# A two-layer graph network on one core: the attention mask of a pair made in four pieces, one for each block of tiles

## Chip, core and metric

The kernel runs on one core of a Trainium2 chip. The metric is the device time of one execution in microseconds (us), as the median of three runs. The profile is one more execution, taken by the hardware profiler.

## What is computed

6250 nodes with 128 features go through two graph layers over 106250 edges that are sorted by destination. The first layer is GATv2 attention, the second a gated message network:

```
h = relu(layernorm(x))
xl, xr = h @ Wl + bl, h @ Wr + br
m = leaky_relu(xl[src] + xr[dst] + edge_attr @ We, 0.2)
logits = m @ att
mx = segment_max(logits, dst)
ex = exp(logits - mx[dst])
out = segment_sum(xl[src] * ex, dst) / segment_sum(ex, dst)
...
em = relu(layer_norm(concat(x[src], x[dst]) @ msg_w + msg_b)) * edge_weight
msgs = segment_sum(em, dst) / counts
...
```

The change lies in the first layer, in the step that takes the maximum of the logits of a destination node over its own edges alone.

## The kernel before

The edges are cut into 64 chunks of 1664 (CH), each of 13 tiles of 128. A pair is one chunk with one window of 125 destination nodes (W) that its edges, sorted by destination, go to. Both layers walk the same list of pairs, 64 in this run. The 13 tiles of a pair fall into four blocks of 4, 3, 3 and 3 tiles (BLK), that is of 512, 384, 384 and 384 columns.

For every tile GpSimd (POOL) issues one indirect DMA that gathers 128 rows of the source table (gather_all, L667): 832 in each layer. They go into a ring of four pairs (xg, U = 4). POOL issues them one after the other; ahead of a block it waits until the sums of the pair four back have been taken (L662), or in the second layer until its messages have been formed.

For a pair in the attention layer, DVE first makes two things from the chunk's destination numbers (dstb, int16, 125 x 1664) and the window's node numbers (node_id, one for each partition). one_hot (L1288) writes oht, 1 in bfloat16 where an edge belongs to the node, and counts them. mask (L1296) writes nmask, 1e30 in float32 where it does not. split_rest and split_low (L1303, L1308) make parts of the window's rows for TensorE. Then the blocks run through a pipeline:

- PE forms the message of a block from oht, the window's parts and the gathered rows (gat_message: L741 three matmuls, L746 transposes that wait for the gathers).
- ACT scales it (gat_low, L982), DVE takes the maximum of both (gat_leaky, L1316), PE makes the logits (L756).
- DVE adds nmask to the logits of the block and takes the smallest over the columns in one instruction (gat_max, L1325, which reads the block's columns of nmask).
- ACT takes the exponential (L991), PE turns it (L764), ACT copies (L1000), PE adds up the sums (L774).
- For the pair two back, gat_merge (L1339 to L1345) and gat_add (L1350 to L1356) fold the results into the node's state.

Each engine's order is written out by hand in a function gat_slot, which runs over the four blocks b of pair k, some stages a few blocks behind. On DVE, slot k holds for each b: gat_leaky of block b, gat_max of the block before, and in between the preparation of pair k + 1: at b = 1 split_rest and one_hot, at b = 2 the mask, at b = 3 split_low. PE starts the messages of pair k + 1 after oht and split_low are there (L736, L737). SP loads the destination numbers of pair k + 2 into the buffer of pair k after DVE is done with the one-hot, the parts and the mask of pair k (L518 to L526). The buffers of dstb, oht and nmask are double.

The second layer has the same form (msg_slot). Its one-hot is L1291, from the same int16 numbers to bfloat16 and without the count. In place of a mask DVE makes 13 small matrices per pair, msg_prob (L1468), in runs of 7 and 6 instructions of 128 x 125.

Of the kernel before, what the change touches and what calls it, by code (L numbers as in the profile page):

```python
# [9 lines left out]
ALU = mybir.AluOpType  # L10
# [3 lines left out]
P = 128  # L14
# [20 lines left out]
BLK = [(0, 4), (4, 7), (7, 10), (10, 13)]  # L35
NB = len(BLK)
# [4 lines left out]
W = 125  # L41
NROW = N + 150
WINDOWS = -(-N // W) + 1
U = 4
# [4 lines left out]
BIG = 1e30  # L49
# [4 lines left out]
def gnn_layers(nc, a, out):  # L54
    with ExitStack() as ctx:
        def sb(name, shape, dt=F32):
            return ctx.enter_context(nc.sbuf_tensor(name, shape, dt))
# [71 lines left out]
        node_id = sb("node_id", [P, 2])  # L129
# [18 lines left out]
        def take(cols):  # L148
            lo = at[0]
            at[0] += cols  # L150
            assert at[0] <= ROOM, at[0]
            return room[:, lo:at[0]]

        xg = take(U * CH).rearrange("p (u e) -> p u e", u=U)
        dstb = take(CH).bitcast(I16).rearrange("p (u e) -> p u e", u=2)
# [5 lines left out]
        nmask = take(2 * CH).rearrange("p (u e) -> p u e", u=2)  # L161
# [180 lines left out]
        def ge(eng, s, v):  # L342
            if type(v) is not int or v > 0:
                eng.wait_ge(s, v)

        def settle(eng):
            eng.sem_inc(s_settled, 1)
# [16 lines left out]
        def turns(s, k, u, ring, n, last):  # L364

            here = (k - u) * (n // ring) + n
            return here + (last + U) * (n // ring) if s.n else here

        def nth(k, b):
            return k * NB + b  # L370

        def value(eng, ap, top):
            settle(eng)
            return nc.values_load(ap, engines=[eng.engine], min_val=0, max_val=top,
                                  skip_runtime_bounds_check_because="the list is built within these bounds")
# [11 lines left out]
        def all_pairs(eng, slot, last, tail):  # L387

            for k in range(U):
                slot(k, k, None)  # L390
            with eng.Fori(U, last, U) as k:
                for u in range(U):
                    slot(k + u, u, None)
            for u in range(U + tail):
                slot(last + u, u % U, u - U)

        def there(k, lag, end):

            if end is not None:
                return end - lag < 0  # L400
            return type(k) is not int or k - lag >= 0
# [27 lines left out]
        def _(sp):  # L429
# [42 lines left out]
            def load_rec(s, k, u):  # L472

                c = value(sp, pair_list[bass.ds(k, 1), 0:1], NCH)
                sp.dma_start(rec[:, u, :].rearrange("p (f t) -> p f t", f=3),
                             rec_rows[bass.ds(c, 1), :, :].rearrange("a f (p t) -> p (a f) t", t=T)).then_inc(s.rec[u], 16)
# [8 lines left out]
            def load_pair(n, s, k, v):  # L485
                c, b = pair_of(k)
                load_dst(s, k, v, c)
                load_window(n, s, v, b)
                return c

            def load_ew(c, v):
                sp.dma_start(oht[W:P, v, :], ew_perm[bass.ds(c, 1), :, :].rearrange("a s e -> (a s) e")).then_inc(gat.ew[v], 16)

            def state_rows(n, b):
                return state0[bass.ds(b, W), :] if n == 0 else state1[bass.ds(b, W), :]

            def width(n):
                return SW if n == 0 else D

            def feed(n, s):  # L500
                def slot(k, u, end):
                    v = u % 2
                    if there(k, 2, end):

                        b = value(sp, pair_list[bass.ds(k - 2, 1), 1:2], N)
                        if there(k, 3, end):
                            sp.wait_ge(s.kept[1 - v], turns(s, k - 3, 1 - v, 2, 16, last))
                            settle(sp)
                        sp.dma_start(st_in[0:W, v, 0:width(n)], state_rows(n, b)).then_inc(s.st[v], 16)
                    if there(k, -3, end):  # L510
                        ge(sp, s.m, nth(k - 1, NB))
                        settle(sp)
                        if n == 1:
                            ge(sp, s.pm, 2 * k)
                            settle(sp)
                        load_rec(s, k + 3, (u + 3) % U)
                    if there(k, -2, end):
                        sp.wait_ge(s.oh, k + 1)  # L518
                        settle(sp)
                        sp.wait_ge(s.split, k + 1)  # L520
                        settle(sp)
                        if n == 0:
                            sp.wait_ge(s.mask, k + 1)
                        else:
                            sp.wait_ge(s.rel, k + 1)
                        settle(sp)  # L526
                        c = load_pair(n, s, k + 2, v)
                        if n == 0:
                            sp.wait_ge(s.m, nth(k + 1, 0))
                            settle(sp)  # L530
                            load_ew(c, v)
                    if there(k, 2, end):
                        sp.wait_ge(s.state, k - 1)
                        settle(sp)
                        sp.dma_start(state_rows(n, b), st_out[0:W, v, 0:width(n)]).then_inc(s.kept[v], 16)

                all_pairs(sp, slot, last, 2)
# [562 lines left out]
        def _(dve):  # L1100
# [171 lines left out]
            def lagged(stage, k, u, b, lag, end):  # L1272
                back = -((b - lag) // NB)
                if there(k, back, end):
                    stage(k - back, (u - back) % U, (b - lag) % NB)
# [14 lines left out]
                else:  # L1290
                    dve.tensor_scalar(oht[0:W, v, :], dstb[0:W, v, :], node_id[0:W, v:v + 1], None, ALU.is_equal).then_inc(s.oh, 1)  # L1291

            def mask(k, u):
                s, v = gat, u % 2
                dve.wait_ge(s.id, k + 1)
                dve.tensor_scalar(nmask[0:W, v, :], dstb[0:W, v, :], node_id[0:W, v:v + 1], BIG, ALU.not_equal,  # L1296
                                  ALU.mult).then_inc(s.mask, 1)

            def split_rest(s, k, u):
# [5 lines left out]
            def split_low(s, k, u):  # L1305
                v = u % 2
                dve.wait_ge(s.mid, k + 1)
                dve.tensor_tensor(dws[0:W, v, 2, :], dres[0:W, :], dws[0:W, v, 1, :], ALU.subtract).then_inc(s.split, 1)  # L1308

            def gat_leaky(k, u, b):  # L1310
                s, c = gat, b % 2
                t0, t1 = BLK[b]
                cols = slice(0, (t1 - t0) * P)
                dve.wait_ge(s.low, nth(k, b) + 1)
                ge(dve, s.logit, nth(k, b) - 1)
                dve.tensor_tensor(act_m[:, c, cols], m_bank[c][:, cols], m_low[:, cols], ALU.max).then_inc(s.act, 1)  # L1316

            def gat_max(k, u, b):
                s, v = gat, u % 2
                t0, t1 = BLK[b]  # L1320
                dve.wait_ge(s.logit, nth(k, b) + 1)
                dve.wait_ge(s.mask, k + 1)
                ge(dve, s.pt, nth(k - 2, b) + 1)
                settle(dve)
                dve.tensor_tensor_reduce(neg_l[0:W, v, t0 * P:t1 * P], logit_bank[b % 2][0:W, 0:(t1 - t0) * P],  # L1325
                                         nmask[0:W, v, t0 * P:t1 * P], 1.0, BIG, ALU.add, ALU.min,
                                         nlocs[0:W, v, b:b + 1]).then_inc(s.negl, 1)
                if b == NB - 1:
                    dve.wait_ge(s.negl, nth(k, NB))
                    ge(dve, s.state, k - 3)  # L1330
                    dve.tensor_reduce(nloc[0:W, u:u + 1], nlocs[0:W, v, :], AX_X, ALU.min).then_inc(s.nloc, 1)  # L1331
# [28 lines left out]
            def gat_slot(k, u, end):  # L1360
                for b in range(NB):
                    if there(k, 0, end):
                        gat_leaky(k, u, b)
                    lagged(gat_max, k, u, b, 1, end)
                    if there(k, -1, end):
                        if b == 1:
                            split_rest(gat, k + 1, (u + 1) % U)
                            one_hot(gat, k + 1, (u + 1) % U)
                        if b == 2:
                            mask(k + 1, (u + 1) % U)  # L1370
                        if b == 3:
                            split_low(gat, k + 1, (u + 1) % U)
                    if there(k, 2, end):
                        if b == 2:
                            gat_merge(k - 2, (u - 2) % U)
                        if b == 3:
                            gat_add(k - 2, (u - 2) % U)

            split_rest(gat, 0, 0)
            one_hot(gat, 0, 0)  # L1380
            mask(0, 0)
            split_low(gat, 0, 0)
            all_pairs(dve, gat_slot, last, 2)

# [224 lines left out]
```

## Time and profile before

| | us |
|---|---|
| median of three runs | 2472.26 (2470.81 to 2472.52) |
| the profiled execution | 2471.0 |
| its span in the trace | 2469.2 |

Busy over the span: POOL 1683.3 us (68%), PE 1646.5 (67%), DVE 1522.7 (62%), PE's weight loads 1201.4 (49%), ACT 982.5 (40%). The first gather of the attention layer starts at 92.3 us, its last ends at 1166.0; those of the message layer run from 1286.0 to 2343.2. Ahead of the first lie the layer norm, the tables and the list of pairs, between them batch norm and the second tables, and behind the second the node update.

How to read it: an engine's busy time leaves out the time in which its sequencer issues and waits, so POOL with 76% busy in a layer can still be without a pause. The cost of an instruction of one engine that stands in the way of another engine's shows in the duration of the latter, not as a wait.

### The profile page before, as it was taken

The page shows a single profiled execution, that of the slowest core. Times are in us where ns is not written, and L with a number is a line of the kernel's source. Part 1 is how long each engine was busy: PE and PEld are TensorE (multiplying, and loading weights), DVE is VectorE, ACT ScalarE, POOL GpSimd, SP SyncE. Part 2 cuts the span into 40 slices and gives each one's busy share as a digit, 9 for nine tenths or more (in the row PEclk, how much of TensorE's full clock was granted, in tenths as well). Part 3 has the DMA queues.
Part 4 walks back from the last instruction along what each step waited for, and adds up shares of the span by engine and source line. Part 5 has one row for each costly group of instructions (what it writes and reads, how often), then busy time and mean ns, then how long its engine had stood idle before and what let it go on. Part 6 is the DMA issues. An engine that isn't in the chain of part 4 may idle for free.

```text
span 2469.2 us, 44266 instructions
## 1 busy us (share of the span) xinstructions
PE 1646.5 (67%) x9934; PEld 1201.4 (49%) x9934; DVE 1522.7 (62%) x4806; ACT 982.5 (40%) x3715; POOL 1683.3 (68%) x1718
## 2 busy tenths in 40 slices
PE   2387778777877777777456666666666666666650
PEld 2255555555555555555344454454454455544550
DVE  5455555555555555555647766666676666667668
ACT  3244334333434343434444444444444344434420
POOL 3377777777777777776017777777777777777732
PEclk9799889898988998999677888888788888889885
DMA  8544344444444344343244444433444444344321
GB/s 257 138 91 86 91 91 87 91 90 90 88 89 91 85 92 89 87 91 72 58 121 98 86 89 92 92 87 89 92 91 86 91 92 92 83 92 93 76 56 52
DMA packets 207823, 228.62 MB, mean 93 GB/s; under 512 B 103103, under 2 KB 153684, under 8 KB 207701
## 3 DMA queue, kind: packets, MB, share of 16 engines
q0 software_dynamic: 54784, 115.94, 24.0%
q1 hardware_dynamic: 152598, 110.34, 16.4%
q10 hardware_dynamic: 384, 1.70, 0.3%
q8 instruction: 20, 0.33, 0.1%
q14 instruction: 37, 0.30, 0.0%
HBM read 194.60 MB, written 33.24 MB: 92 GB/s over the span
## 4 chain that ended last, share of the span: by engine, by line
POOL 56%; issue 19%; PE 8%; DMA 7%; DVE 5%; SPq 1%; ACT 1%; POOLq 1%; ACTq 0%; DVEq 0%
POOL room L667 56%; DMA room<-src_table,rec 5%; PE psum L774 2%; PE psum L704 1%; PE psum L756 1%; PE psum L746 1%; DMA node_x<-in_x 1%; DVE room L1557 1%; PE psum L741 1%; DMA room<-state 1%; DVE stats L1127 1%; PE psum L835 1%; SPq L457 1%; PE psum L764 0%; ACT room L1000 0%
## 5 line engine op out<-in xcount | busy, mean ns | idle before, releaser
L667 POOL DMA_INDIRECT room<-src_table,rec x1664 | 1624.4, 976 | 684.1 <-issue 495.3
L835 PE MATMUL psum<-room,ident 128*128 128x384 f32 (+1 forms) x512 | 292.6, 659 | 377.4 <-DMA room<-src_table,rec 297.9
L1050 ACT ACTIVATE room<-psum 128x128 f32<-128x128 f32 x832 | 218.8, 274 | 585.6 <-DVE room L1478 583.2
L1316 DVE TENSOR_TENSOR room<-psum,room 128x384 f32<-128x384 f32 (+1 forms) x256 | 151.1, 590 | 455.6 <-ACT room L982 367.8
L982 ACT ACTIVATE room<-psum 128x384 f32<-128x384 f32 (+1 forms) x256 | 132.1, 516 | 560.5 <-PE psum L746 557.4
L1478 DVE TENSOR_TENSOR room<-psum,msg_g 128x384 f32<-128x384 f32 (+1 forms) x256 | 151.0, 590 | 315.0 <-PE psum L840 312.8
L746 PE MATMUL psum<-ident,room 128*128 128x128 f32 x832 | 155.4, 305 | 207.4 <-DMA room<-src_table,rec 206.9
L835 PEld LDWEIGHTS psum<-room,ident 128*128 128x128 f32 x512 | 93.1, 227 | 409.7 <-issue 384.7
L853 PE MATMUL psum<-room 128*125 128x128 f32 x1664 | 285.2, 318 | 1.5 <-ACT room L1062 1.5
L774 PE MATMUL psum<-room 128*125 128x128 f32 x1664 | 262.2, 300 | 18.9 <-ACT room L1000 6.3
L840 PEld LDWEIGHTS psum<-room 125*128 125x128 bf16 x2496 | 195.4, 112 | 140.8 <-issue 123.8
L774 PEld LDWEIGHTS psum<-room 128*125 128x125 f32 x1664 | 222.6, 204 | 56.4 <-ACT room L1000 54.5
L853 PEld LDWEIGHTS psum<-room 128*125 128x125 f32 x1664 | 248.7, 225 | 2.1 <-ACT room L1062 2.1
L1492 DVE SCALAR_TENSOR_TENSOR room<-room,rstd_e,msg_beta 128x128 f32<-128x128 f32 x832 | 243.0, 349 | 10.2
L746 PEld LDWEIGHTS psum<-ident,room 128*128 128x128 f32 x832 | 107.5, 155 | 280.5 <-DMA room<-src_table,rec 263.4
L756 PE MATMUL psum<-room,natt 128*125 128x384 f32 (+1 forms) x512 | 242.0, 557 | 1.8 <-DVE room L1316 1.8
L1468 DVE TENSOR_SCALAR room<-iota_w,rel,rec 128x125 f32<-128x125 f32 x832 | 225.2, 362 | 0.0
L840 PE MATMUL psum<-room 125*128 125x128 bf16 x2496 | 218.2, 244 | 0.0
L741 PE MATMUL psum<-room 128*128 128x384 bf16 (+1 forms) x768 | 190.5, 360 | 38.8 <-DVE room L1308 33.4
L991 ACT ACTIVATE room<-room,nloc 125x384 f32<-125x384 f32 (+1 forms) x256 | 163.8, 640 | 73.1 <-DVE nloc L1331 69.3
L1050 ACT ACTIVATION_READ_ACCUMULATOR room<-psum 128x1 f32 x832 | 168.8, 203 | 0.0
L764 PEld LDWEIGHTS psum<-ident,room 125*128 125x128 f32 x832 | 115.7, 152 | 108.0 <-issue 79.0
(179 smaller groups left out, 2122.6 us busy)
## 6 DMA issues: line engine op xcount, KB each, us to landing
room<-dst_perm SPq DMA_DIRECT2D x128, 406.2 KB
room<-src_table,rec POOLq DMA_INDIRECT x1664
room<-dst_table SPq DMA_DIRECT2D x128, 62.5 KB
src_table<-room SPq DMA_DIRECT2D x24, 224.0 KB
dst_table<-room SPq DMA_DIRECT2D x24, 224.0 KB
st_in<-state SPq DMA_DIRECT2D x64, 64.0 KB
state<-st_out SPq DMA_DIRECT2D x64, 64.0 KB
st_in<-state SPq DMA_DIRECT2D x64, 62.5 KB
```

The source lines that it names most:

```text
L667: pool.indirect_dma_start(out=xg[:, u, t * P:(t + 1) * P], out_offset=None, in_=src_table[n][:, :], in_offset=bass.IndirectOffsetOnAxis(ap ...
L741: nc.tensor.matmul(m_bank[c][:, cols], dws[:, v, p, :], oht[:, v, t0 * P:t1 * P], start=(p == 0), stop=False, skip_group_check=True)
L746: i = nc.tensor.matmul(m_bank[c][:, j * P:(j + 1) * P], xg[:, u, t * P:(t + 1) * P], ident[:, :], start=False, stop=(t == t1 - 1), is_tran ...
L756: nc.tensor.matmul(logit_bank[c][0:W, cols], natt[:, :], act_m[:, c, cols], start=True, stop=True).then_inc(s.logit, 1)
L774: i = nc.tensor.matmul(sum_bank[u % 2][0:W, 0:D], prob[:, c, t - t0, 0:W], xg[:, u, t * P:(t + 1) * P], start=(t == 0), stop=(t == T - 1), ...
L835: nc.tensor.matmul(msg_bank[b][:, cols], ident[:, :], xg[:, u, t0 * P:t1 * P], start=True, stop=False, skip_group_check=True)
L840: i = nc.tensor.matmul(msg_bank[b][:, j * P:(j + 1) * P], oht[0:W, v, t * P:(t + 1) * P], dws[0:W, v, p, :], start=False, stop=(t == t1 - ...
L853: i = nc.tensor.matmul(sum_bank[u % 2][0:W, 0:D], pm[:, u % 2, t, 0:W], zr[:, b, j * P:(j + 1) * P], start=(t == 0), stop=(t == T - 1), sk ...
L991: nc.scalar.activation(prob_wt[0:W, b % 2, 0:(t1 - t0) * P], neg_l[0:W, u % 2, t0 * P:t1 * P], ACT.Exp, bias=nloc[0:W, u:u + 1], scale=-1. ...
L1050: i = nc.scalar.activation(sq[:, j * P:(j + 1) * P], msg_bank[b][:, j * P:(j + 1) * P], ACT.Square, accum_out=var_e[:, c, j:j + 1])
L1468: i = dve.tensor_scalar(pm[:, v, t, 0:W], iota_w[:, :], rel[:, v, t:t + 1], rec[:, u, 2 * T + t:2 * T + t + 1], ALU.is_equal, ALU.mult)
L1492: i = dve.scalar_tensor_tensor(out=xz[:, c, j * P:(j + 1) * P], in0=hgs[:, c, j * P:(j + 1) * P], scalar=rstd_e[:, c, j:j + 1], in1=msg_be ...
```

## The change

mask takes a block number b and writes that block's columns alone, from the same columns of dstb. Pieces 0 and 1 (512 and 384 columns) stand at b = 2 of the slot, where the whole mask stood, pieces 2 and 3 (384 each) at b = 3, ahead of split_low. The semaphore mask now counts four for a pair. gat_max waits for its own block's piece, and SP for all four. The prologue makes the four pieces of pair 0 in a row.

```diff
--- before.py
+++ after.py
@@ -520,7 +520,7 @@
                         sp.wait_ge(s.split, k + 1)
                         settle(sp)
                         if n == 0:
-                            sp.wait_ge(s.mask, k + 1)
+                            sp.wait_ge(s.mask, nth(k + 1, 0))
                         else:
                             sp.wait_ge(s.rel, k + 1)
                         settle(sp)
@@ -1290,10 +1290,11 @@
                 else:
                     dve.tensor_scalar(oht[0:W, v, :], dstb[0:W, v, :], node_id[0:W, v:v + 1], None, ALU.is_equal).then_inc(s.oh, 1)
 
-            def mask(k, u):
+            def mask(k, u, b):
                 s, v = gat, u % 2
+                cols = slice(BLK[b][0] * P, BLK[b][1] * P)
                 dve.wait_ge(s.id, k + 1)
-                dve.tensor_scalar(nmask[0:W, v, :], dstb[0:W, v, :], node_id[0:W, v:v + 1], BIG, ALU.not_equal,
+                dve.tensor_scalar(nmask[0:W, v, cols], dstb[0:W, v, cols], node_id[0:W, v:v + 1], BIG, ALU.not_equal,
                                   ALU.mult).then_inc(s.mask, 1)
 
             def split_rest(s, k, u):
@@ -1319,7 +1320,7 @@
                 s, v = gat, u % 2
                 t0, t1 = BLK[b]
                 dve.wait_ge(s.logit, nth(k, b) + 1)
-                dve.wait_ge(s.mask, k + 1)
+                dve.wait_ge(s.mask, nth(k, b + 1))
                 ge(dve, s.pt, nth(k - 2, b) + 1)
                 settle(dve)
                 dve.tensor_tensor_reduce(neg_l[0:W, v, t0 * P:t1 * P], logit_bank[b % 2][0:W, 0:(t1 - t0) * P],
@@ -1366,8 +1367,9 @@
                         if b == 1:
                             split_rest(gat, k + 1, (u + 1) % U)
                             one_hot(gat, k + 1, (u + 1) % U)
-                        if b == 2:
-                            mask(k + 1, (u + 1) % U)
+                        if b >= 2:
+                            mask(k + 1, (u + 1) % U, 2 * b - 4)
+                            mask(k + 1, (u + 1) % U, 2 * b - 3)
                         if b == 3:
                             split_low(gat, k + 1, (u + 1) % U)
                     if there(k, 2, end):
@@ -1378,7 +1380,8 @@
 
             split_rest(gat, 0, 0)
             one_hot(gat, 0, 0)
-            mask(0, 0)
+            for b in range(NB):
+                mask(0, 0, b)
             split_low(gat, 0, 0)
             all_pairs(dve, gat_slot, last, 2)
 
```

The order of DVE at the slot's b = 2 inside the loop. Names: room is the large tile in which dstb, nmask and the like lie, st_out, st_in and shift belong to gat_merge. Before:

```order
L1325 ISA nlocs 125x1
L1296 TENSOR_SCALAR room<-room,node_id 125x1664 [waits id0]
L1339 TENSOR_TENSOR st_out<-st_in,nloc 125x1 [waits esh0,st_1,nloc0]
L1341 TENSOR_TENSOR st_out<-st_in,cloc 125x1
L1344 TENSOR_TENSOR shift<-st_out,st_in 125x1 [waits nnew0]
```

and of the change:

```order
L1326 ISA nlocs 125x1
L1297 TENSOR_SCALAR room<-room,node_id 125x512 [waits id0]
L1297 TENSOR_SCALAR room<-room,node_id 125x384 [waits id0]
L1340 TENSOR_TENSOR st_out<-st_in,nloc 125x1 [waits esh0,st_1,nloc0]
L1342 TENSOR_TENSOR st_out<-st_in,cloc 125x1
L1345 TENSOR_TENSOR shift<-st_out,st_in 125x1 [waits nnew0]
```

One instruction of 1664 columns has become two of 512 and 384, back to back, at the same place. Lines behind L1293 have moved by one.

The order of DVE at b = 3 of the same slot, where L1308 (L1309) is split_low. Before:

```order
L1316 TENSOR_TENSOR room<-psum,room 128x384 [waits logit0,low0]
L344 REGISTER_ALU [waits mask0,logit0]
L1325 ISA room,nlocs<-psum,room 125x384 [waits pt0]
L1325 ISA nlocs 125x1
L1308 TENSOR_TENSOR room<-room 125x128 [waits mid0]
L1350 TENSOR_REDUCE den<-dens 125x1 [waits sum0]
```

and of the change:

```order
L1317 TENSOR_TENSOR room<-psum,room 128x384 [waits logit0,low0]
L344 REGISTER_ALU [waits mask0,logit0]
L1326 ISA room,nlocs<-psum,room 125x384 [waits pt0]
L1326 ISA nlocs 125x1
L1297 TENSOR_SCALAR room<-room,node_id 125x384 [waits id0] x2
L1309 TENSOR_TENSOR room<-room 125x128 [waits mid0]
L1351 TENSOR_REDUCE den<-dens 125x1 [waits sum0]
```

Two instructions of 384 columns now stand ahead of split_low. The orders of the other engines are the same in both.

## Rows read from the trace of the kernel before

**Rows 1.** Busy time of POOL's gathers by layer (windows of line L667): count in brackets

```profile
core 0: us, POOL busy (x), PEclk, DMA share, GB/s
92.20:1166.10 1073.90, 820.46 (x832) 0.91 0.41 89
1285.90:2343.30 1057.40, 803.96 (x832) 0.83 0.41 90
```

**Rows 2.** Line L667 in the attention layer: duration ns min/median/max; idle time before by cause

```profile
L667 POOL DMA_INDIRECT room<-src_table,rec x832: 940/944/1782, 92.3 to 1165.1; - x167
...
  issue: 245.3, 805
...
  PE psum L774: 7.9, 26
```

**Rows 3.** Line L667 in the message layer, same columns

```profile
L667 POOL DMA_INDIRECT room<-src_table,rec x832: 940/944/1350, 1286.0 to 2342.3; - x167
...
  issue: 249.9, 820
```

**Rows 4.** Groups of DVE by form: busy us, mean ns | idle before

```profile
L1468 DVE TENSOR_SCALAR room<-iota_w,rel,rec 128x125 f32<-128x125 f32 x832 | 225.2, 362 | 0.0
L1288 DVE TENSOR_SCALAR_CACHE_REDUCE room<-room,node_id 125x1664 bf16<-125x1664 int16 x64 | 124.6, 1946 | 2.3
...
L1291 DVE TENSOR_SCALAR room<-room,node_id 125x1664 bf16<-125x1664 int16 x64 | 42.4, 662 | 2.3
```

**Rows 5.** Lines of DVE, each by itself: duration ns min/median/max, first and last start

```profile
L1296 DVE TENSOR_SCALAR room<-room,node_id x64: 1078/1083/1298, 110.6 to 1149.8; 125x1664 f32<-125x1664 int16 x64
...
L1291 DVE TENSOR_SCALAR room<-room,node_id x64: 652/654/719, 1301.2 to 2325.4; 125x1664 bf16<-125x1664 int16 x64
...
L1468 DVE TENSOR_SCALAR room<-iota_w,rel,rec x832: 327/341/545, 1301.9 to 2333.3; 128x125 f32<-128x125 f32 x167
```

**Rows 6.** Timeline (start us, us, engine line): a gather that starts inside a mask

```profile
527.72 1.08 DVE L1296 TENSOR_SCALAR room<-room,node_id 125x1664 f32<-125x1664 int16 x1
...
527.97 1.65 POOL L667 DMA_INDIRECT room<-src_table,rec  x1 [0.30 <-issue]
...
528.71 0.15 DVE L1339 TENSOR_TENSOR st_out<-st_in,nloc 125x1 f32<-125x1 f32 x1
```

**Rows 7.** Timeline: a gather that was under way when the mask started

```profile
512.29 1.62 POOL L667 DMA_INDIRECT room<-src_table,rec  x1 [0.30 <-issue]
...
512.71 1.08 DVE L1296 TENSOR_SCALAR room<-room,node_id 125x1664 f32<-125x1664 int16 x1
```

**Rows 8.** Timeline: a gather half done when the mask starts, and the next

```profile
159.42 0.94 POOL L667 DMA_INDIRECT room<-src_table,rec  x1 [0.30 <-issue]
...
159.91 1.30 DVE L1296 TENSOR_SCALAR room<-room,node_id 125x1664 f32<-125x1664 int16 x1
...
160.66 1.36 POOL L667 DMA_INDIRECT room<-src_table,rec  x1 [0.30 <-PE psum L774]
```

**Rows 9.** Timeline, message layer: a gather that starts inside L1291

```profile
1309.54 0.65 DVE L1291 TENSOR_SCALAR room<-room,node_id 125x1664 bf16<-125x1664 int16 x1
1309.83 1.18 POOL L667 DMA_INDIRECT room<-src_table,rec  x1 [0.30 <-issue]
```

**Rows 10.** Timeline, message layer: a gather inside a run of seven L1468

```profile
1650.21 1.86 DVE L1468 TENSOR_SCALAR room<-iota_w,rel,rec 128x125 f32<-128x125 f32 x7
...
1650.95 0.95 POOL L667 DMA_INDIRECT room<-src_table,rec  x1 [0.30 <-issue]
```

**Rows 11.** Timeline: end of a slot, from gat_max to the next pair's first matmuls

```profile
619.12 0.92 PE L774 MATMUL psum<-room 128*125 128x128 f32 x6
...
619.58 0.29 DVE L1308 TENSOR_TENSOR room<-room 125x128 bf16<-125x128 f32 x1
...
620.06 0.82 PE L741 MATMUL psum<-room 128*128 128x512 bf16 x3
```

**Rows 12.** Waits of the attention layer (108 to 1160 us): us in total, times, longest

```profile
PE psum L746 <- DMA room<-src_table,rec: 205.7, 111, 5.3
```

## Prediction

> **What bounds the kernel now.** I first read the gathers by layer [rows 1]. POOL issues 832 in each; busy time is 820.5 us in the attention layer, 986 ns each, and 804.0 in the message layer, 966 each. Beside that stand the pauses [rows 2]: 0.30 us ahead of each gather (245.3/805), all of them the sequencer's own; the 26 put down to PE are as short (7.9/26). 832 x 0.305 is 253.8, and 820.5 + 253.8 = 1074.3, which is the layer's whole stretch of 1073.9. So POOL issues without one pause from 92.3 to 1166.1 us, everything else in the layer follows it, and a nanosecond off a gather there is a nanosecond off the kernel. What follows starts when the layer is done, so it moves along.
>
> The gathers should all be alike: least 940, median 944 ns, yet the longest takes 1782 [rows 2]. 832 x 0.944 is 785.4, so 35.1 us are excess. The message layer has 18.6 of it and a longest of 1350 [rows 3].
>
> The timeline says where the excess is. At 527.97 a gather starts 0.25 us into a mask and takes 1.65 us [rows 6]. One that was 0.42 us old when the mask began takes 1.62 [rows 7]. One that was 0.49 old takes 0.94, but there the mask takes 1.30 in place of 1.08, and the next gather, 0.75 us into the mask, takes 1.36 [rows 8]. So the mask and the gathers exclude each other for a time. I went through all 64 masks, from 110.6 to 1149.8 us, this way: 90 gathers overlap one, with 33.7 us above 943 ns between them, 0.53 per mask. The other 742 have 2.2 us in all. Nearly all of the layer's excess comes from this one instruction.
>
> **What an instruction costs the gathers.** The rows give rules, with D an instruction's duration. A gather that starts over 0.1 us after it ends at its end + 0.82: 528.80 + 0.82 = 529.62 in [rows 6], 161.21 + 0.82 = 162.03 in [rows 8], and for L1291 1310.19 + 0.82 = 1311.01 in [rows 9]. Its loss is D - y - 0.12, y being how late it starts. A gather that is x old at that time, x under 0.45, ends at the instruction's end + 0.12 (513.79 + 0.12 = 513.91 in [rows 7]); its loss is x + D - 0.82. A gather older than that loses nothing. The worst loss is about D - 0.22, and below a D of 0.37 the second kind vanishes. With the gathers' period of 1.25 us and phases spread evenly, the mean for D = 1.08 comes to 0.51 us; 0.53 was found. The cost grows nearly with the square of D.
>
> How long will a piece be? The fp32 mask of 1664 columns takes 1.083, L1291 with bfloat16 output 0.654 and the counting L1288 1.946 [rows 4, 5]. These fit 0.225 + 0.858, 0.225 + 0.429 and 0.225 + 1.716: a fixed part, and columns at 1, 2 and 1/2 of the mask's rate. A piece of 512 then takes 0.225 + 0.264 = 0.489, one of 384 0.225 + 0.198 = 0.423. The next instruction starts 0.09 before the end (528.71 against 528.80 in [rows 6]).
>
> To price a piece I use what three lines cost the gathers, by the column part h: L1296, h = 0.858, 0.53 us each; L1291, h = 0.429, 9.4 us over 64, 0.147 each; L1468, h near 0.065, 6.05 us over 832, 0.0073 each. A curve a h + b h^2 through the first two has a = 0.07, b = 0.63 and gives 0.0072 for the third, which it wasn't fitted to. So 384 columns cost 0.039, 512 cost 0.063.
>
> L1468 also answers the question whether pieces back to back act as one long hold. It comes in runs of 7 that last 1.86 us, and a gather in the middle of one takes 0.95 [rows 10]; its durations reach 545 ns against 341 [rows 5], so it does exclude gathers but lets them in between two instructions.
>
> The Trainium skill, SBUF — State Buffer, "SBUF: two separate sides", has a rule for this: GpSimd and a VectorE instruction in a 2-port mode share a port pair that whoever starts first keeps for its whole instruction, and the other waits. The trace agrees on the exclusion. It doesn't agree on "whole": a gather past its middle isn't stopped [rows 8]. What the page's rule would give is the second rival.
>
> **The sum.** *Removed:* 64 masks at 0.527 = 33.7 us of POOL's path. *Added:* per pair 0.063 + 3 x 0.039 = 0.18, times 64 = 11.5 us. The bounds are 0 (every piece falls where it harms nothing) and 18.9 (each two pieces as one hold: h = 0.462 and 0.396 by the curve, 0.168 + 0.128 = 0.296 per pair). I take 11.5, since [rows 10] are the nearest to pieces in a run. Net -22.2 us.
>
> *DVE:* start to start the mask took 0.99; the pieces take 0.40 + 3 x 0.33 = 1.39, so 0.40 x 64 = 26 us more. DVE is busy 587 of the layer's 1074 us and waits for what the gathers bring; its cover is that. *Moved:* 0.67 us of mask now stand ahead of split_low, on which PE's next pair hangs. In [rows 11] split_low ends at 619.87 and PE starts the pair at 620.06, having been busy until 620.04; now it would start near 620.7. That is 0.67 x 64 = 43 us of PE, covered by the 205.7 us in which PE waits for gathers [rows 12], 3.2 per pair, and by the ring, which lets POOL run on some ten blocks ahead of the sums. If that cover were gone, the 43 us would be on the path. *SP:* it waits for the last piece in place of the mask, but it already waited for split_low of the same pair, which stands behind both; its loads start 0.67 us later, a slot (16 us) ahead of their use. Nothing. *Waits:* gat_max waits for its own piece, made most of a slot earlier. Nothing. *Prologue:* 0.4 us of DVE once, while POOL gathers. Nothing.
>
> The profiled execution took 2471.0 (its span 2469.2): 2471.0 - 22.2 = 2448.8. The median of the runs is 1.3 above it: **2450 us**. Bounds alone: 33.7 - 18.9 and 33.7 - 0 give 2457.5 and 2438.6.
>
> **Rivals.** *Two pieces hold as one.* For: they follow each other on DVE with nothing in between. Against: [rows 10]. 2457.5. Chance 0.11.
>
> *Each piece stops gathers for its whole length.* Then a gather that starts in a piece waits until its end, and the loss is D^2/2 over the period: (0.489^2 + 3 x 0.423^2)/2.5 = 0.31 per pair, 19.9 us, against 1.083^2/2.5 = 0.47, 30.0 us, for the mask: 10.1 us less, 2462. (This is the rule of the Trainium skill's page named above.) Against: it gives 30.0 where the trace has 33.7, and [rows 8]. Chance 0.08.
>
> *The pieces don't run as the mask did.* A piece of 384 at half the mask's rate, that of L1288, would take 0.62 and exclude nothing, as L1288 does (its gathers are among the 742): 2439. Against: the pieces have even counts and the same types as the mask. Chance 0.03.
>
> *The pieces keep step with the gathers: slower.* DVE's work in a block starts when the block's last gather has landed, so the phase needn't be spread evenly. If each of the four pieces starts just before a gather does, each costs D - 0.22: 0.27 + 3 x 0.20 = 0.87 per pair, 56 us against 33.7, so +22 us, 2494. It turns slower above 0.13 us per piece, three times my mean. Against: in the masks of [rows 6 to 8] the phases differ (0.25 after, 0.42 and 0.49 before), and four pieces at two places can't all be unlucky for long. Chance 0.06.
>
> *PE becomes the bound*: the 43 us don't vanish in its waits, because these are uneven (up to 5.3 us at a time). POOL would then show pauses, and the gain would be eaten: about 2472, or a little more. Against: the ring's depth. Chance 0.05.
>
> **How the numbers follow.** Forecast 0.67. Faster by over 0.2% (4.9 us, about what a measurement of this kernel can tell from no change) are the forecast and the first three rivals: 0.67 + 0.11 + 0.08 + 0.03 = 0.89. The last rival gives 0.04 to the same and 0.01 to slower, with the one before it 0.07. The range goes from the bound at 2439 to the second rival at 2462, and leaves out some 0.12.
>
> **What to look for.** Gathers of the attention layer: busy 798 us in place of 820.5, mean 960 ns; the longest, 1782, gone, and nothing above 1.3. POOL's stretch 1052 us, its pauses still 0.30. Pieces of about 0.42 and 0.49 us, some stretched by gathers. PE's wait for gathers lower by some 40 to 65 us. The message layer unchanged at 804. Wrong would be: gathers of 1.5 us around two pieces (held as one), pauses on POOL above 0.31 (PE's), or a stage 1074 us long in spite of shorter gathers.

## Result and profile after

| | before | after |
|---|---|---|
| median of four runs, us | 2471.53 | 2443.57 (2442.83 to 2448.17) |
| span of the profiled execution | 2469.2 | 2441.0 |

The ratio is 0.9892, with a 95% interval of 0.9875 to 0.9909: the kernel is 1.1% faster. 2450 was predicted, 2439 to 2462 the range. Among the experiments below, one of the six executions of mask_on_act took 2470.9 us at a mean granted TensorE clock of 0.63; the other five had 0.85 and took 2438.0 to 2442.2, and the one widens that kernel's interval.

The windows of POOL's gathers, each layer from its first to its last, answer to [rows 1]:

```profile
core 0: us, POOL busy (x), PEclk, DMA share, GB/s
91.30:1138.80 1047.50, 794.03 (x832) 0.92 0.42 91
1257.90:2313.60 1055.70, 802.20 (x832) 0.82 0.41 90
```

The attention layer's 832 gathers take 794.0 us in place of 820.5, and the layer is as much shorter: 1047.5 against 1073.9. The message layer, in which nothing was edited, differs by 1.8 us. These two are the 28.2 us of the span.

Line L667 in the attention layer, with its idle time by cause, against [rows 2]:

```profile
L667 POOL DMA_INDIRECT room<-src_table,rec x832: 940/944/1191, 91.4 to 1137.7; - x167
...
  issue: 246.2, 808
...
  PE psum L774: 7.0, 23
```

The median gather is the same, 944 ns; the longest fell from 1782 to 1191. The pauses are still 0.30 us each, so POOL still sets the pace. The excess (busy time above that of as many undisturbed gathers) over 832 x 0.944 = 785.4 fell from 35.1 to 8.6 us.

The pieces, as a line of DVE (duration ns min/median/max):

```profile
L1297 DVE TENSOR_SCALAR room<-room,node_id x256: 399/416/652, 110.6 to 1126.2; 125x512 f32<-125x512 int16 x64, 125x384 f32<-125x384 int16 x64
```

And the timeline with a gather inside the first of two pieces, DVE's row and POOL's:

```profile
893.24 0.81 DVE L1297 TENSOR_SCALAR room<-room,node_id 125x512 f32<-125x512 int16 x2
...
893.42 1.11 POOL L667 DMA_INDIRECT room<-src_table,rec  x1 [0.30 <-issue]
```

The first piece alone takes 0.48 us, from 893.24 to 893.72, and 893.72 + 0.82 = 894.54 against the gather's end at 894.53. It is the rule of [rows 6], with the end of the first piece: the second doesn't count. Inside a whole mask a gather that started 0.25 us late took 1.65.

What PE waited for, gathers and then split_low (L1309), against [rows 11, 12] (us in total, times, longest):

```profile
PE psum L746 <- DMA room<-src_table,rec: 157.3, 98, 5.6
...
PE psum L741 <- DVE room L1309: 54.8, 26, 34.3
```

And the wait for split_low in the kernel before:

```profile
PE psum L741 <- DVE room L1308: 33.4, 1, 33.4
```

PE's waits for gathers shrank by 48 us. The long wait for split_low is the one at the layer's start, 33.4 us before and 34.3 now. The other 25 waits, 20.5 us in all, are new. So the late split_low is real, and POOL's unchanged pauses show that it is covered.

### The profile page after: what moved, and what is told of

Its sections match the earlier page's. It is cut to its first block, busy times and chain, and to the rows that moved or that the text cites. A ratio compares the mean times of both kernels' runs of the same rounds, so it can differ in the third digit from the quotient of the medians.

```text
span 2441.0 us, 44458 instructions
## 1 busy us (share of the span) xinstructions
PE 1632.4 (67%) x9934; PEld 1191.2 (49%) x9934; DVE 1554.4 (64%) x4998; ACT 979.6 (40%) x3715; POOL 1655.1 (68%) x1718
## 4 chain that ended last, share of the span: by engine, by line
POOL 55%; issue 19%; PE 9%; DMA 8%; DVE 5%; ACT 1%; SPq 1%; POOLq 1%; ACTq 0%; DVEq 0%
POOL room L667 55%; DMA room<-src_table,rec 5%; PE psum L704 2%; PE psum L774 2%; PE psum L835 1%; PE psum L746 1%; DMA node_x<-in_x 1%; DVE room L1560 1%; PE psum L756 1%; DVE stats L1127 1%; PE psum L840 1%; DMA room<-state 1%; PE psum L741 1%; PE psum L853 0%; ACT room L1000 0%
## 5 line engine op out<-in xcount | busy, mean ns | idle before, releaser
L667 POOL DMA_INDIRECT room<-src_table,rec x1664 | 1596.2, 959 | 683.1 <-issue 496.2
L853 PEld LDWEIGHTS psum<-room 128*125 128x125 f32 x1664 | 249.9, 226 | 1.5 <-ACT room L1062 1.5
L774 PEld LDWEIGHTS psum<-room 128*125 128x125 f32 x1664 | 216.4, 199 | 56.5 <-ACT room L1000 52.6
L741 PE MATMUL psum<-room 128*128 128x384 bf16 (+1 forms) x768 | 185.2, 352 | 79.6 <-DVE room L1309 54.8
```

The lines of the kernel that those rows point to most:

```text
L667: pool.indirect_dma_start(out=xg[:, u, t * P:(t + 1) * P], out_offset=None, in_=src_table[n][:, :], in_offset=bass.IndirectOffsetOnAxis(ap ...
L741: nc.tensor.matmul(m_bank[c][:, cols], dws[:, v, p, :], oht[:, v, t0 * P:t1 * P], start=(p == 0), stop=False, skip_group_check=True)
L774: i = nc.tensor.matmul(sum_bank[u % 2][0:W, 0:D], prob[:, c, t - t0, 0:W], xg[:, u, t * P:(t + 1) * P], start=(t == 0), stop=(t == T - 1), ...
L853: i = nc.tensor.matmul(sum_bank[u % 2][0:W, 0:D], pm[:, u % 2, t, 0:W], zr[:, b, j * P:(j + 1) * P], start=(t == 0), stop=(t == T - 1), sk ...
```

## Experiments

All kernels below share one edit outside the loops: the two counts that are loaded at the start are checked against their bounds.

```diff
-            turns_left = nc.values_load(counts[0:1, 0:1], engines=[eng.engine], min_val=NCH - 3 * U, max_val=NCH * WINDOWS,
-                                        skip_runtime_bounds_check_because="each chunk has 1 to WINDOWS pairs")
+            turns_left = nc.values_load(counts[0:1, 0:1], engines=[eng.engine], min_val=NCH - 3 * U, max_val=NCH * WINDOWS)
```

and likewise for the count of blocks. With it the line numbers move by one or two. The kernels were run in three groups on three chips, those of the first two groups once each, and chips differ: the kernel before took 2471.2 us beside whole_bounded to thirteen_pieces, 2467.6 beside four_at_2 to message_counted, and 2474.1 beside the last three. So the comparisons go by the traces of the two layers first, and by the total second.

One more difference has to be known when busy times are compared. In most traces the median gather takes 944 ns. In before_split_low_late, message_counted, mask_on_act and mask_on_act_message_counted it takes 947, in both layers, for no reason that the edits give. This is mask_on_act's line in the attention layer:

```profile
L666 POOL DMA_INDIRECT room<-src_table,rec x832: 941/947/1073, 92.9 to 1133.9; - x167
```

Over 832 gathers these 3 ns are 2.5 us of busy time that belong to no DVE instruction.

### whole_bounded: the base

> The kernel before, with the two loaded counts (pairs, blocks) checked against their bounds once per engine ahead of the loops; every further kernel has this too, so this is their base. Every theory: no difference. Gathers of the attention layer busy 820 us (818 to 823), of the message layer 804, time within 3 us of the kernel before.

2470.1 us, beside 2471.2 for the kernel before on the same chip. Gathers busy 819.8 and 802.4 us. The check costs nothing that can be seen.

### counted_mask: a whole mask in the counting form

```diff
-                dve.tensor_scalar(nmask[0:W, v, :], dstb[0:W, v, :], node_id[0:W, v:v + 1], BIG, ALU.not_equal,
-                                  ALU.mult).then_inc(s.mask, 1)
+                dve.tensor_scalar(nmask[0:W, v, :], dstb[0:W, v, :], node_id[0:W, v:v + 1], None, ALU.not_equal, ALU.add,
+                                  accum_out=mcount[0:W, :]).then_inc(s.mask, 1)
```

> The whole mask in one instruction at its old place, but in the form of L1288 (compare and count): it writes 0 and 1 in place of 0 and 1e30, so the output isn't the reference's. It takes DVE 1.95 us in place of 1.08. Theory (an instruction at double rate shuts the gathers out while it runs, one in the counting form doesn't): the excess falls from 35 to about 2 us, gathers of the attention layer busy 788 us, time about 2437, below even the four pieces, although DVE works longer than in either. Rival (what counts is how long DVE is busy, or how long one of its instructions is, whatever its form): excess above 35 us, about 60, busy about 845, time 2495.

2437.4 us. The windows of its gathers in both layers, its line L666, and the timeline of one mask with two gathers:

```profile
92.70:1132.10 1039.40, 786.07 (x832) 0.93 0.43 92
1253.10:2308.10 1055.00, 801.66 (x832) 0.84 0.41 90
```

```profile
L666 POOL DMA_INDIRECT room<-src_table,rec x832: 940/944/1062, 92.7 to 1131.1; - x167
```

```profile
122.80 1.94 DVE L1295 TENSOR_SCALAR_CACHE_REDUCE room<-room,node_id 125x1664 f32<-125x1664 int16 x1
...
122.83 0.94 POOL L666 DMA_INDIRECT room<-src_table,rec  x1 [0.30 <-issue]
124.07 0.94 POOL L666 DMA_INDIRECT room<-src_table,rec  x1 [0.30 <-issue]
```

An instruction with the same input and the same shape and type of output, nearly twice as long, and two gathers pass through it at 0.94 us each. Excess 0.7 us. Length alone doesn't stop the gathers; it counts only in a form that does. That settles where the 35 us came from; the layer's floor is 786.

### two_pieces

```diff
-            def mask(k, u, b):
+            def mask(k, u, h):
                 s, v = gat, u % 2
-                cols = slice(BLK[b][0] * P, BLK[b][1] * P)
+                cols = slice(0, 896) if h == 0 else slice(896, CH)
...
                         if b >= 2:
-                            mask(k + 1, (u + 1) % U, 2 * b - 4)
-                            mask(k + 1, (u + 1) % U, 2 * b - 3)
+                            mask(k + 1, (u + 1) % U, b - 2)
```

(The waits of gat_max and SP and the prologue count two pieces in place of four.)

> Two pieces of 896 and 768 columns, the first at b = 2, the second at b = 3. Theory (cost by the length of one hold, by the curve of the prediction): 0.168 + 0.128 us per pair, 19 us in all, busy about 805 us, time about 2455. If two pieces back to back held as one, this would be the same as the four pieces measured (busy 794). If the gain came from taking DVE work out of b = 2 and not from short holds, busy also about 794.

2448.7 us, its gathers and its pieces:

```profile
93.50:1145.70 1052.20, 798.73 (x832) 0.92 0.42 91
```

```profile
L1295 DVE TENSOR_SCALAR room<-room,node_id x128: 610/681/851, 111.6 to 1132.8; 125x896 f32<-125x896 int16 x64, 125x768 f32<-125x768 int16 x64
```

Between one piece and four, as the theory has it: 798.7 us of gathers, 4.7 above the four. But the excess is 13.3 us where the curve gave 19, and the time is 6 us below the expected 2455: the curve is too high in its middle.

### thirteen_pieces

```diff
-                dve.tensor_scalar(nmask[0:W, v, cols], dstb[0:W, v, cols], node_id[0:W, v:v + 1], BIG, ALU.not_equal,
-                                  ALU.mult).then_inc(s.mask, 1)
+                for t in range(*BLK[b]):
+                    i = dve.tensor_scalar(nmask[0:W, v, t * P:(t + 1) * P], dstb[0:W, v, t * P:(t + 1) * P], node_id[0:W, v:v + 1], BIG,
+                                          ALU.not_equal, ALU.mult)
+                i.then_inc(s.mask, 1)
```

(The line that sets cols goes too.)

> Thirteen pieces of 128 columns, 7 at b = 2 and 6 at b = 3. Theory: the column part of one is 0.066 us, like L1468's, at 0.0075 us each 0.1 per pair, 6 us in all; busy 788 to 792. DVE's mask costs 13 x 0.21 = 2.7 us per pair in place of 1.4, of which 1.3 ahead of split_low, in place of 0.67; if PE's waits cover it, time 2438 to 2442. Rival (more instructions, more meetings with a gather, each at a fixed price): 13/4 of the excess of the four pieces, 28 us, busy 813, time 2463. Rival (PE becomes the bound by the late split_low): pauses above 0.31 us on POOL, time above 2450 with busy at 790.

2440.9 us:

```profile
92.80:1136.20 1043.40, 790.06 (x832) 0.89 0.43 92
```

```profile
L1295 DVE TENSOR_SCALAR room<-room,node_id x832: 266/281/505, 110.6 to 1124.8; 125x128 f32<-125x128 int16 x167
```

Three times as many instructions as the change, and the excess is 4.7 us in place of 8.6. A fixed price per meeting is out: it would have been 28.

### four_at_2: do pieces back to back hold as one?

```diff
-                        if b >= 2:
-                            mask(k + 1, (u + 1) % U, 2 * b - 4)
-                            mask(k + 1, (u + 1) % U, 2 * b - 3)
+                        if b == 2:
+                            for c in range(NB):
+                                mask(k + 1, (u + 1) % U, c)
```

> The change with all four pieces in one run at b = 2, none ahead of split_low. Theory (each piece is a hold by itself, gathers get in between, also within a run of four): by the rules of the prediction 0.16 us per pair, against 0.15 for the change's two runs of two; busy of the attention layer's gathers 793 to 797, time within 3 us of the change. Rival (back to back they shut the gathers out as one): their hold would be as long as that of the whole mask, busy about 825 to 840, time about 2475 to 2490. If the lateness of split_low had cost the change anything, this one would be faster than it with the same busy time.

2440.1 us. Its two layers:

```profile
92.60:1139.00 1046.40, 793.06 (x832) 0.91 0.42 91
1258.60:2310.60 1052.00, 798.56 (x832) 0.84 0.42 90
```

Four in a run are no worse than two and two: 793.1 against 794.0. So gathers do get in between two pieces; what shortens the hold is the cut, not the distance. The total is 3.5 us below the change's median, 0.5 more than expected, but the message layer, which has no edit, is 3.7 us shorter (1052.0 against 1055.7). Over the runs without an edit there its gathers' busy time varies from 798.6 to 804.0 us. The attention layers are alike (1046.4 and 1047.5), so where split_low stands cost the change nothing that can be seen.

### before_split_low_late and change_split_low_3us: the cover on PE

```diff
                         if b == 3:
+                            for _ in range(1):
+                                dve.tensor_reduce(idle[0:PP, :], node_x[:, 0:4, :].rearrange("p t f -> p (t f)"), AX_X, ALU.max)
                             split_low(gat, k + 1, (u + 1) % U)
```

(0:21 in place of 0:4 for the second, on top of the change.)

> The kernel before (whole mask) with one more DVE instruction ahead of split_low in each slot, a maximum over 512 columns of node_x that nothing uses, about 0.7 us: it puts split_low off as the change does and does nothing else. Theory (PE's waits for gathers cover it): POOL's pauses stay at 0.30, time within 2 us of the kernel before. Rival (the late split_low costs part of the change's gain): up to 0.7 x 64 = 43 us slower, POOL pauses above 0.31.

2474.6 us, where the kernel before took 2467.6 beside it and whole_bounded 2470.1 on another chip: outside the 2 us that were expected. But the trace has its attention layer as it was:

```profile
94.00:1167.70 1073.70, 820.25 (x832) 0.91 0.41 89
1287.90:2345.10 1057.20, 803.68 (x832) 0.83 0.42 90
```

1073.7 and 1057.2 us, against 1073.9 and 1057.4 in [rows 1]. The span, 2472.8, is 3.6 us longer than that of the kernel before: 1.8 of them lie ahead of the first gather and 1.8 behind the last, where the edit doesn't reach. The run of 2467.6 has no trace, so where the rest of the 7 us lies isn't known. The extra instruction took 0.68 us. So a split_low that much later costs nothing in the layer, though the time alone doesn't show it.

> The change with such an instruction over 2688 columns, about 3.0 us, ahead of split_low: the point from which that wait decides. PE waits 157 us for gathers in the changed kernel, 2.5 us per pair, of which the mean is used up by 3.0. Theory (cover by PE's waits plus the ring of four pairs): the overshoot of some 0.5 us per pair costs at most 32 us, and the ring takes some of it up: 2446 to 2476, with pauses on POOL for the first time. Rival (there is much more cover than PE's waits show): within 2 us of the change, no pauses. Rival (little cover): 3.0 x 64 = 190 us, 2630.

2477.0 us. The extra instruction takes 2.94 us. Its windows, its gathers' causes, and the wait between the layers:

```profile
91.60:1146.20 1054.60, 792.91 (x832) 0.87 0.42 90
1295.90:2349.30 1053.40, 800.07 (x832) 0.83 0.41 90
```

```profile
POOL room L666 <- PE psum L773: 16.9, 38, 1.8
...
PE psum L740 <- DVE room L1308: 139.5, 30, 32.9
```

```profile
POOL room L666 <- DMA rec<-rec_rows: 149.8, 1, 149.8
```

The gathers themselves are as short as the change's (792.9), yet the run is 33.5 us slower than the change, and 37 slower than four_at_2 on the same chip. POOL now pauses for PE's sums, up to 1.8 us, and the layer grows by 7 us. The greater part is not there: between the layers POOL waits 149.8 us, where the change has 119.4. PE's last sums (L773) end 42 us after the last gather, where in the change they end 14 us after it: PE has fallen 28 us further behind. It waits for no gather any more. With 2.9 us more the cover is gone; with the change's 0.7 it is not. The time is 1 us above the expected range, which had counted on POOL's pauses to show the loss.

### message_counted

```diff
-                if s is gat:
-                    dve.tensor_scalar(oht[0:W, v, :], dstb[0:W, v, :], node_id[0:W, v:v + 1], None, ALU.is_equal, ALU.add,
-                                      accum_out=cloc[0:W, u:u + 1]).then_inc(s.oh, 1)
-                else:
-                    dve.tensor_scalar(oht[0:W, v, :], dstb[0:W, v, :], node_id[0:W, v:v + 1], None, ALU.is_equal).then_inc(s.oh, 1)
+                dve.tensor_scalar(oht[0:W, v, :], dstb[0:W, v, :], node_id[0:W, v:v + 1], None, ALU.is_equal, ALU.add,
+                                  accum_out=cloc[0:W, u:u + 1]).then_inc(s.oh, 1)
```

> The change, and in the message layer the one-hot (L1292, 0.65 us at quadruple rate) in the counting form of L1288, 1.95 us; the count isn't used there. Theory (a hold vanishes, 9.4 us of excess were counted around L1291): busy of the message layer's gathers 793 in place of 802, time about 2435, if DVE's 1.3 us more per pair (busy 717 of 1057 us before) are covered. Rival (DVE or PE becomes the bound there): POOL pauses above 0.31 in the message layer, time 2444 or more.

2440.5 us:

```profile
92.00:1141.80 1049.80, 796.26 (x832) 0.91 0.42 91
1262.70:2312.60 1049.90, 796.47 (x832) 0.85 0.40 90
```

The message layer's gathers fall to 796.5, below all runs without this edit, though DVE works 1.3 us longer per pair there. It is 5.7 us under the change, or some 7.5 when each trace is taken against its own undisturbed gathers (the median is 947 ns here), and not the 9.4 that I had put down to L1291. The gathers that overlap the counting one-hot here still have 2.8 us of excess, so that part wasn't L1291's. The attention layer took 2.2 us more than the change's, nearly all of it by the 947 ns, so little is left in the total, and the expected 2435 was missed.

### change_bounded, mask_on_act, and both edits: a faster version

The mask comes from ACT, out of the one-hot, as 1e30 - 1e30 * oht, at b = 2 and 3; DVE makes none:

```diff
+            def gat_mask(k, u, b):
+                s, v = gat, u % 2
+                cols = slice(BLK[b][0] * P, BLK[b][1] * P)
+                act.wait_ge(s.oh, k + 1)
+                ge(act, s.negl, nth(k - 2, NB))
+                nc.scalar.activation(nmask[0:W, v, cols], oht[0:W, v, cols], ACT.Identity, bias=big_col[0:W, :],
+                                     scale=-BIG).then_inc(s.mask, 1)
...
                     lagged(gat_exp, k, u, b, 4, end)
+                    if b >= 2 and there(k, -1, end):
+                        gat_mask(k + 1, (u + 1) % U, 2 * b - 4)
+                        gat_mask(k + 1, (u + 1) % U, 2 * b - 3)
```

(Not shown: big_col, a column of 1e30; the prologue's four pieces; and SP, which no longer waits for the mask, since that no longer reads the destination numbers.)

> The changed kernel with the two loaded counts checked against their bounds, the base for the other two in this call. Every theory: the change's time, 2443.6, within 4 us; attention layer's gathers busy 794, message layer's 802.

> The mask made by ACT from the one-hot as 1e30 - 1e30 * oht, in four pieces at b = 2 and 3, in place of DVE. Theory (only DVE's double-rate instruction shuts the gathers out, ACT doesn't): excess of the attention layer as with the counting form, busy 786 to 788, DVE 1.4 us per pair shorter, ACT about 2.0 us per pair longer (ACT's copies of 384 columns take 0.49), 426 to about 555 busy of 1040 us. If that is covered, 2436 to 2438. Rival (ACT's 1 us more ahead of gat_low of the next block makes PE late): PE's waits for gathers shrink, POOL pauses, 2444 or more.

> Both: mask by ACT, and the message layer's one-hot in the counting form, which alone took 5.7 us off that layer's gathers (796.5 against 802.2). Theory: the savings lie in different layers and add up: 2443.6 - 7 - 6 = 2431 (2428 to 2434). Rival (the message layer's gain was scatter between runs, whose message layers differ by 3.6 us without any edit there): same as mask_on_act.

| | median us | ratio to before | 95% interval |
|---|---|---|---|
| before | 2474.09 | | |
| change_bounded | 2448.38 | 0.9896 | 0.9882 to 0.9911 |
| mask_on_act | 2439.77 | 0.9885 | 0.9847 to 0.9923 |
| mask_on_act_message_counted | 2434.08 | 0.9835 | 0.9822 to 0.9848 |

On this chip both kernels are 3 to 5 us slower than on the first, so the three times are 2 to 5 us above what was expected (change_bounded 4.8, mask_on_act 1.8 above 2438, both edits 3.1 above 2431, at the upper end of the range). Five of mask_on_act's six executions lie below the fastest of change_bounded's four (2443.9). The traces show where, in the attention layer; first mask_on_act's windows, then those of both edits:

```profile
92.90:1134.80 1041.90, 788.44 (x832) 0.91 0.42 92
1253.70:2310.40 1056.70, 803.25 (x832) 0.83 0.41 90
```

```profile
91.80:1133.90 1042.10, 788.57 (x832) 0.91 0.42 92
1254.20:2304.00 1049.80, 796.34 (x832) 0.84 0.41 90
```

788.4 in place of 794.0 with ACT's mask, and 2.5 of these 788.4 are the 947 ns again, so its true excess is near counted_mask's. In the message layer the counting form gives 796.3 once more, against 803.3 in mask_on_act, whose gathers have the same median: 6.9 us. The two savings add up. DVE's busy time in the attention layer falls from 614 to 520 us, ACT's rises from 424 to 559 and stays covered. ACT's pieces of 384 take 0.61 us, not the 0.49 of its copies.

## Why the prediction was right, point by point

- *POOL bounds the layer without a pause, so an excess nanosecond is a nanosecond of the kernel.* Right: excess and stretch fell together, 26.5 and 26.4 us, and the pauses stayed at 0.30. In change_split_low_3us, where that no longer holds, the gathers are short and the kernel is slow.
- *The excess comes from the mask.* Shown by counted_mask: 0.7 us is left of 35.1, so the mask's part is 34.4, where 33.7 was counted.
- *Gathers get in between back-to-back pieces* (first rival: they hold as one). Shown by four_at_2.
- *The price of a piece.* This is the term that was mis-sized, 11.5 us for the four. The excess is 8.6, and 7.9 over the floor of counted_mask: 0.12 per pair, not 0.18. The step behind it is the curve a h + b h^2. Its second point was too high: L1291's 0.147 each counted all excess of gathers that overlap it, and taking its hold away gave 5.7 to 7.5 us, 0.09 to 0.12 each. The rest belongs to neighbours, and which of them wasn't tried. But mending that point doesn't mend the curve: through 0.11 it would have a negative a and price the four pieces at 4 us, below what they cost. The form itself was wrong. By the prediction's own rules the loss goes with the square of D - 0.22 and not of D.

The rules of the single rows alone, with losses D - y - 0.12 and x + D - 0.82, do better. I applied them in two ways: averaged over evenly spread phases, and gather by gather with the phases that each trace has. Measured are the excess over 785.4 less the 0.7 of counted_mask, and the excess of only those gathers that overlap a piece, over the trace's undisturbed mean of 943.5 ns (all in us):

| mask | D us | rules, even phases | layer's excess | rules, trace's phases | overlapping gathers |
|---|---|---|---|---|---|
| one (whole_bounded) | 1.08 | 31 | 33.7 | 33.0 | 33.3 |
| two | 0.68, 0.61 | 13 | 12.6 | 13.4 | 12.8 |
| four (the change) | 0.48, 3 x 0.42 | 5 | 7.9 | 8.6 | 8.6 |
| thirteen | 0.28 | 1 | 4.0 | 0.6 | 3.5 |

(For one: ((1.08 - 0.22)^2 / 2 + (0.71^2 - 0.16^2) / 2) / 1.25 x 64 = 31, which is 0.49 per mask; the prediction has 0.51.) With the phases of the trace the rules give the change's cost with nothing left over in the sum (7.6 against 7.7 in change_bounded, 6.6 against 6.9 in four_at_2). What they lack with even phases is thus the phases: 64 times in the change a gather starts inside a piece at a point where it loses, and evenly spread they would be 47. Why the phases bunch wasn't tried. Only for thirteen pieces do some 3 us remain that the rules don't have, and their cause is open.

- *The second rival, by the page's rule*: each piece stops a gather for its whole length, 19.9 us and a time of 2462. Out: 7.9 us. The Trainium skill, SBUF — State Buffer, "SBUF: two separate sides", names the exclusion and its partners rightly. The same page, "Who interferes with whom", says of tensor_scalar that the form which also writes out its accumulator doesn't run in a 2-port mode; counted_mask agrees (0.7 us of excess). The page's "for the whole instruction" holds here for DVE's instruction and not for a gather: one that had started first was stopped all the same at 0.42 us of its age [rows 7], and one that was 0.49 us old held the mask up by 0.22 us only, while it had 0.45 still to run [rows 8].
- *Phases in step, slower*: none of the four arrangements (two, four, four in a run, thirteen) is slower. Its premise was partly true all the same: the phases aren't evenly spread, which costs the change some 3 us by the table above.
- *PE's cover.* Right for 0.7 us. With 2.9 us more it is gone, so its bound lies between. PE's mean wait of 2.5 us per pair in the change fits that. The lag at the layer's end, and not only POOL's pauses, has to be counted.
- *The duration of the pieces, 0.489 and 0.423 us*: measured 0.483 and 0.415 (medians).
- The remaining difference, 2450 against 2443.6: 4.2 us from the gathers' busy time (26.4 less in place of 22.2), 1.8 from the message layer, which has no edit and for which nothing was forecast (luck, and to the fast side), and 0.5 from the step between the profiled execution and the median, 0.7 in place of 1.3.

## What to carry to other kernels

Where GpSimd issues gathers without a pause, look at the longest gather beside the median, and find on the timeline which DVE instruction lies over the long ones. If it is one at double or quadruple rate from SBUF to SBUF, cut it, put it into a form without that rate if the result allows it, or give it to ACT. Here the loss per instruction fell from 0.53 to 0.10 and 0.03 us as the duration went from 1.08 to 0.65 and 0.43, faster than with its square, and thirteen pieces still had less excess than four (4.7 against 8.6). That DVE takes longer for the same work is no loss while it isn't the engine that others wait for. A first measure of that slack is the mean wait of the next engine, and a lag may surface only at the end of a stage. Before busy times of two traces are compared, compare their medians too: 3 ns over 832 gathers are 2.5 us.

## What the hardware showed unexpectedly

- A slower instruction made the kernel faster: 1.94 us in place of 1.08, and 2437 in place of 2470.
- A gather and a double-rate instruction don't exclude each other for all their length. In the change's trace no gather older than 0.48 us of its 0.94 is delayed by a piece that starts then (four between 0.46 and 0.48 lose 0.05 to 0.12 us, three of them after an earlier piece, so the prediction's 0.45 isn't sharp). The piece is stretched instead if the gather is younger than some 0.7 us, from 0.48 to at most 0.65 (the maximum of L1297), as the mask was from 1.08 to 1.30 [rows 8].
- In change_split_low_3us a stage lost some 37 us, of which only 7 showed in the stretch of the engine that paces it. The other 30 were a lag that became visible when the last gather was done.
